# Self-attention of a routed transformer layer: keys rotated ahead of queries, norms in two parts, logits in other banks

## The reference

```python
x = x + xattn(layernorm(x), ctx)      # one head, 257 keys, width 384 to 512
x = x + attn(layernorm(x), ...)       # 16 heads of 32, rotary embedding, 32 keys
x = x + ffn(layernorm(x), ...)        # 8 experts of 1024, the best 2 per token
```

```python
q, k, v = x @ Wq.T + bq, x @ Wk.T + bk, x @ Wv.T + bv      # (B, T, 16, 32)
q, k = apply_rope(q), apply_rope(k)   # [x1*cos - x2*sin, x1*sin + x2*cos]
attn = softmax(einsum('bthd,bshd->bhts', q, k) / sqrt(32))
out = einsum('bhts,bshd->bthd', attn, v).reshape(B, T, C) @ Wo.T + bo
```

## Time and profile before

| what | value |
|---|---|
| median of 3 runs | 589.7 us (588.83 to 590.61) |
| the profiled execution, timed | 589.92 us |
| its span in the profile | 588.0 us |
| mean granted TensorE clock | 0.935 of full |
| busy: TensorE, VectorE, ScalarE, GpSimd | 506.1, 391.0, 285.9, 113.1 us |
| chain that ended last | TensorE 67%, VectorE 10%, issue 10%, ScalarE 5%, GpSimd 3%, DMA 3% |

### The profile page before, as it was taken

How to read it: one execution, slowest core, us unless ns; L and a number is a source line. 1 busy time by engine, 2 the same in 40 slices (tenths; PEclk the granted TensorE clock), 3 DMA queues, 4 the chain that set the end, 5 groups by cost and what they waited for, 6 DMA issues and landing times.

```text
span 588.0 us, 11090 instructions
## 1 busy us (share of the span) xinstructions
PE 506.1 (86%) x3601; PEld 294.6 (50%) x3602; DVE 391.0 (67%) x876; ACT 285.9 (49%) x449; POOL 113.1 (19%) x89
## 2 busy tenths in 40 slices
PE   5799999999989899886630699999999999999993
PEld 3664657474657576645330344445445444544441
DVE  2889778937977969698886566666563736673330
ACT  0652868686256464675720345454443525652120
POOL 1212114102232030300471001211211121121112
PEclk9799999999989989897855779999999999999998
DMA  8992505000008994125288157887585776744222
GB/s 326 390 382 87 216 1 215 2 1 2 1 0 303 379 382 172 37 80 208 90 299 294 44 174 223 267 255 237 107 262 132 218 214 154 232 93 90 54 54 37
DMA packets 54961, 98.74 MB, mean 168 GB/s; under 512 B 25072, under 2 KB 26256, under 8 KB 50832
## 3 DMA queue, kind: packets, MB, share of 16 engines
q1 hardware_dynamic: 23984, 74.81, 35.9%
q10 hardware_dynamic: 26640, 13.73, 9.5%
q0 software_dynamic: 4304, 9.77, 7.8%
HBM read 63.36 MB, written 29.43 MB: 158 GB/s over the span
## 4 chain that ended last, share of the span: by engine, by line
PE 67%; DVE 10%; issue 10%; ACT 5%; POOL 3%; DMA 3%; SPq 0%; ACTq 0%; POOLq 0%; DVEq 0%
PE bank L691 20%; PE bank L709 19%; PE bank L343 7%; PE bank L511 4%; PE bank L495 2%; PE bank L425 2%; PE bank L455 2%; PE bank L405 2%; PE bank L361 2%; PE bank L476 1%; PE bank L545 1%; ACT ctxT_region L737 1%; DMA routed_rows<-shared,ints 1%; POOL small L1544 1%; PE bank L604 1%
## 5 line engine op out<-in xcount | busy, mean ns | idle before, releaser
L691 PE MATMUL bank<-wbuf,ctx_region 128*128 x504 | 117.8, 393 | 6.3 <-issue 5.3
L1400 DVE SCALAR_TENSOR_TENSOR wbuf<-ctx_region,wbuf 128x2048 f32 (+1 forms) x28 | 62.9, 2288 | 31.9 <-ACT wbuf L876 31.9
L1642 POOL DMA_INDIRECT out<-misc,ints x21 | 38.6, 1840 | 230.2 <-ACT misc L957 175.0
L691 PEld LDWEIGHTS bank<-wbuf,ctx_region 128*128 128x128 f16 x504 | 49.4, 101 | 66.9 <-issue 15.5
L876 ACT ACTIVATE wbuf<-ctx_region 128x2048 f32 (+1 forms) x28 | 51.9, 1902 | 28.6 <-issue 26.2
L1544 POOL TENSOR_TENSOR small<-small 128x2 f32<-128x2 f32 (+2 forms) x25 | 27.7, 1109 | 190.8 <-DVE small L1030 184.2
L709 PE MATMUL bank<-wbuf,actT 128*128 x264 | 58.8, 379 | 1.0 <-DVE actT L1504 1.0
L976 ACT ACTIVATE ctxT_region<-bank 128x512 f32<-128x512 f32 x42 | 25.1, 597 | 69.6 <-PE bank L691 69.6
L709 PE MATMUL bank<-wbuf,xn 128*128 x240 | 53.4, 379 | 0.0
L511 PE MATMUL bank<-ctx_region,wbuf 128*128 128x256 f16 x384 | 45.2, 280 | 4.3 <-DVE ctx_region L1159 3.4
L511 PEld LDWEIGHTS bank<-ctx_region,wbuf 128*128 128x128 f16 x384 | 38.0, 100 | 12.0 <-DVE ctx_region L1159 4.1
(11 more groups left out here) (214 smaller groups left out, 823.4 us busy)
## 6 DMA issues: line engine op xcount, KB each, us to landing
ctx_region<-in_experts SPq DMA_DIRECT2D x28, 1024.0 KB, 5.4
routed_rows<-ctxT_region SPq DMA_DIRECT2D x1, 16900.0 KB, 50.6
ctx_region<-in_ctx SPq DMA_DIRECT2D x8, 1536.0 KB, 8.8
ctx_region<-routed_rows ACTq DMA_DIRECT2D x23, 260.0 KB, 3.6
wbuf<-in_experts SPq DMA_DIRECT2D x4, 1024.0 KB, 4.9
out<-x ACTq DMA_DIRECT2D x8, 256.0 KB, 2.5
x<-in_x SPq DMA_DIRECT2D x1, 1536.0 KB, 14.3
wbuf<-in_wqT SPq DMA_DIRECT2D x4, 256.0 KB, 4.3
```

What stands on the lines that cost most here:

```text
L691: mm = nc.tensor.matmul(bank[half][:, :], xgT[:, b, x_part, k * P:(k + 1) * P], w16[:, ds(at + (w_part + k * EH + half * 512), 512)], star ...
L1400: nc.vector.scalar_tensor_tensor(w16[:, ds(at + (LOW + n * PIECE), PIECE)], src_[:, piece], W_SCALE, w16[:, ds(at + (HIGH + n * PIECE), PI ...
L1642: nc.gpsimd.indirect_dma_start(out, bass.IndirectOffsetOnAxis(idx[:, slot_no:slot_no + 1].bitcast(U32), axis=0), y_out[:, slot_no, :], Non ...
```

## The change

On VectorE the keys of the next pair are rotated before its queries. `first_norm` is split in `first_stats`, ahead of the keys' rotation, and `first_scale`, behind it. The queries' shuffle and cosine (`turn_cos`) stand before `attended_low`, their sine (`turn_sin`) behind `normalised_low`, and their sum (`join`) between the statistics (`last_stats`) and the scaling (`last_scale`) of the last norm. `logits_out` stands behind the keys' rotation and the scaling, in the pass before the last behind both rotations. On TensorE the scores go ahead of `features_T`, and the values ahead of the logits; the first two pairs' logits go to banks 4 and 5. On ScalarE the exponentials come first, then the queries' copies, then the features'. Waits follow the new order: `scores` wait for both sums, `key_columns` for the first of the two, `values` for the feature copies, `attend` for the queries' copies, and the output products of passes 1 and 2 for the last pair's logits sum (z). The first pair keeps its order.

```diff
--- before.py
+++ after.py
@@ -43,7 +43,7 @@
 PIECE = EXPERT // W_PIECES
 ROW_SLOTS = 2
 ROUTED = ((0, TILES - 4), (TILES - 4, TILES - 2), (TILES - 2, TILES))
-LOGIT_BANK = (2, 2, 6, 2)
+LOGIT_BANK = (4, 4, 6, 2)
 COUNT_BANKS = ((0, 1), (0, 1), (0, 1))
 
 
@@ -525,6 +525,8 @@
 
             def values(pair):
                 pe.wait_ge(s["sw_lo"], 3)
+                if pair > 1:
+                    pe.wait_ge(s["xfT"], 2 * pair - 2)
                 if pair:
                     pe.wait_ge(s["sv"], 2 * pair)
                 else:
@@ -537,7 +539,7 @@
                     mm.then_inc(s["sv_ps"], 1)
 
             def scores(pair):
-                pe.wait_ge(s["rotated"], 2 * pair + 1)
+                pe.wait_ge(s["rotated"], 2 * pair + 2 if pair else 1)
                 pe.wait_ge(s["k_exp"], pair + 1)
                 for t in range(2):
                     for c4 in range(KC):
@@ -558,8 +560,8 @@
 
             def attend(pair):
 
-                if pair:
-                    pe.wait_ge(s["z"], min(2 * pair, TILES - 4))
+                if pair + 1 < PAIRS:
+                    pe.wait_ge(s["sq"], 2 * pair + 4)
                 for t in range(2):
                     pe.wait_ge(s["p_cols"], 2 * pair + t + 1)
                     pe.wait_ge(s["sv"], 2 * pair + t + 1)
@@ -577,6 +579,8 @@
                     normalised_T(pair + 2)
                 if pair == 0:
                     pe.wait_ge(s["sw_lo"], 4)
+                elif pair + 1 < PAIRS:
+                    pe.wait_ge(s["z"], 2 * pair)
                 for t in range(2):
                     pe.wait_ge(s["ao_hi"], 2 * pair + t + 1)
                     for k in range(KC):
@@ -597,7 +601,7 @@
 
             def logits(pair):
                 if pair + 2 < PAIRS:
-                    pe.wait_ge(s["sq"], 2 * pair + 6)
+                    pe.wait_ge(s["sk"], 2 * pair + 6)
                 for t in range(2):
                     pe.wait_ge(s["xfT"], 2 * pair + t + 1)
                     for k in range(KC):
@@ -647,13 +651,13 @@
                     logits(pair - 1)
                 else:
                     queries(pair + 1)
+                    scores(pair)
                     if pair:
                         features_T(pair - 1)
-                    scores(pair)
                     keys(pair + 1)
+                    values(pair + 1)
                     if pair:
                         logits(pair - 1)
-                    values(pair + 1)
                 attend(pair)
             pe.wait_ge(s["z"], TILES - 2)
             features_T(PAIRS - 1)
@@ -883,7 +887,7 @@
 
             def key_columns(pair):
 
-                act.wait_ge(s["rotated"], 2 * pair + 2)
+                act.wait_ge(s["rotated"], 2 * pair + 1 if pair else 2)
                 for r in range(4):
                     part = slice(r * HD, (r + 1) * HD)
                     op = nc.scalar.copy(k_exp[part, :, :, r, :], kbuf[part].rearrange("p (c b l) -> p c b l", c=KC, l=L))
@@ -908,22 +912,22 @@
             key_columns(0)
             for pair in range(PAIRS):
                 last = pair + 1 == PAIRS
+                if last:
+                    gate_exp(0)
+                for t in range(2):
+                    act.wait_ge(s["s_sub"], 2 * pair + t + 1)
+                    nc.scalar.activation(soft[:, t, :], soft[:, t, :], ACT.Exp, scale=H_SCALE).then_inc(s["s_exp"], 1)
+                if not last:
+                    turned_out(pair + 1)
                 if pair and not last:
                     features_out(pair - 1)
                     features_high(pair - 1)
-                if not last:
-                    turned_out(pair + 1)
-                for t in range(2):
-                    act.wait_ge(s["s_sub"], 2 * pair + t + 1)
-                    nc.scalar.activation(soft[:, t, :], soft[:, t, :], ACT.Exp, scale=H_SCALE).then_inc(s["s_exp"], 1)
                 if last:
                     features_out(pair - 1)
                     probs_out(pair)
                 else:
                     biased(k_T, 4, s["sk_ps"], 2 * pair + 2, "sbk", s["sk"])
                     probs_out(pair)
-                    if pair + 2 == PAIRS:
-                        gate_exp(0)
                     values_out(pair + 1)
                 for t in range(2):
                     act.wait_ge(s["ao_ps"], 2 * pair + t + 1)
@@ -1035,14 +1039,6 @@
             def x_at(tile):
                 return x[:, tile * D:(tile + 1) * D]
 
-            def norm_pair(srcs, dsts, name, pair):
-                norm_stats(srcs, stats, mv, ve, s[f"{name}_ve"])
-                dve.wait_ge(s[f"{name}_rstd"], pair + 1)
-                out_sem = s[f"{name}_out"]
-                for t in range(2):
-                    normalise(dsts[t], srcs[t], mv[:, t, 0:1], rstd[:, t:t + 1]).then_inc(out_sem, 1)
-                dve.wait_ge(out_sem, 2 * pair + 2)
-
             count(nc.vector.memset(neg_half, -0.5), "route", wait=False)
             dve.wait_ge(s["x_in0"], 16)
 
@@ -1146,11 +1142,21 @@
                     nc.vector.tensor_tensor(x2a[:, 1, :, tile_at], x2aT[:, :, tile_at], x2a[:, 0, :, tile_at], ALU.subtract)\
                         .then_inc(s["x2a_lo"], 1)
 
-            def first_norm(pair):
+            def first_stats(pair):
+                dve.wait_ge(s["x_new"], 2 * pair + 2)
+                norm_stats([x_at(2 * pair), x_at(2 * pair + 1)], stats, mv, ve, s["ln3_ve"])
+
+            def first_scale(pair):
+                dve.wait_ge(s["ln3_rstd"], pair + 1)
                 if pair == 0:
                     dve.wait_ge(s["x1T_ps"], TILES)
-                dve.wait_ge(s["x_new"], 2 * pair + 2)
-                norm_pair([x_at(2 * pair), x_at(2 * pair + 1)], [xn[:, 0, :], xn[:, 1, :]], "ln3", pair)
+                for t in range(2):
+                    normalise(xn[:, t, :], x_at(2 * pair + t), mv[:, t, 0:1], rstd[:, t:t + 1]).then_inc(s["ln3_out"], 1)
+                dve.wait_ge(s["ln3_out"], 2 * pair + 2)
+
+            def first_norm(pair):
+                first_stats(pair)
+                first_scale(pair)
 
             def normalised_low(pair):
                 for t in range(2):
@@ -1268,19 +1274,30 @@
             cos_t = const("cos")[:, None, :].to_broadcast(table)
             turned = ((qb, q_sw, s["sq"]), (kbuf, k_sw, s["sk"]))
 
-            def turn(pair, n):
+            def nth(pair, n):
+
+                return 2 * pair + (2 - n if pair else n + 1)
+
+            def turn_cos(pair, n):
 
                 buf, sw, ready = turned[n]
                 dve.wait_ge(ready, 2 * pair + 2)
                 nc.vector.stream_shuffle(sw, buf, swap).then_inc(s["swapped"], 1)
-                dve.wait_ge(s["swapped"], 2 * pair + n + 1)
+                dve.wait_ge(s["swapped"], nth(pair, n))
                 nc.vector.tensor_tensor(by_place(buf), by_place(buf), cos_t, ALU.mult).then_inc(s["cosined"], 1)
+
+            def turn_sin(n):
+                sw = turned[n][1]
                 nc.vector.tensor_tensor(by_place(sw), by_place(sw), sin_t, ALU.mult).then_inc(s["sined"], 1)
+
+            def turn(pair, n):
+                turn_cos(pair, n)
+                turn_sin(n)
 
             def join(pair, n):
                 buf, sw, _ = turned[n]
-                dve.wait_ge(s["cosined"], 2 * pair + n + 1)
-                dve.wait_ge(s["sined"], 2 * pair + n + 1)
+                dve.wait_ge(s["cosined"], nth(pair, n))
+                dve.wait_ge(s["sined"], nth(pair, n))
                 nc.vector.tensor_tensor(buf, buf, sw, ALU.add).then_inc(s["rotated"], 1)
 
             def attended_low(pair):
@@ -1312,7 +1329,7 @@
                         dve.wait_ge(s["p_cols"], 2 * pair + t - 1)
                     nc.vector.transpose(soft_T[:, t, :], soft[:, t, :]).then_inc(s["s_pT"], 1)
 
-            def last_norm(pair):
+            def last_stats(pair):
 
                 for t in range(2):
                     tile = 2 * pair + t
@@ -1323,6 +1340,8 @@
                     dve.wait_ge(s["x_post"], tile + 1)
                     count(nc.vector.bn_stats(stats[:, t, :], x_at(tile)), "norm_step", wait=(t == 1))
                 norm_mean(stats, mv, ve, s["ln4_ve"], 2)
+
+            def last_scale(pair):
                 dve.wait_ge(s["ln4_rstd"], pair + 1)
                 if pair:
                     dve.wait_ge(s["xf_lo"], 2 * pair)
@@ -1415,24 +1434,30 @@
                 softmax(pair)
                 if last:
                     choose(0)
+                if pair + 2 < PAIRS:
+                    first_stats(pair + 2)
+                if not last:
+                    turn(pair + 1, 1)
+                    join(pair + 1, 1)
+                if pair + 2 < PAIRS:
+                    first_scale(pair + 2)
+                if pair + 2 == PAIRS:
+                    turn(pair + 1, 0)
+                    join(pair + 1, 0)
                 if pair:
                     logits_out(pair - 1)
                 if pair + 2 < PAIRS:
-                    first_norm(pair + 2)
-                if not last:
```

(14 more changed lines are left out.)

## The result

The changed kernel takes 585.05 us (median of 18 runs, 582.57 to 586.34) against 588.73 us for the kernel before (18 runs, 585.29 to 591.7): ratio 0.9939, with a 95% interval of [0.9918, 0.996], 3.6 us faster. The forecast was 583.5, the range 581.0 to 586.8. The profiled execution took 584.41 us, with a mean granted clock of 0.937.

The account below looks back on a forecast made before the run. Bound: TensorE idle stretches of 2.88 us, waiting on a normalisation, then slow-clock scores in two passes; VectorE bounds the third. Terms: -7.6 + 1.4 = -6.2; 589.92 - 6.2 = 583.7, median 583.5 us; range 581.0 to 586.8.

Parts of the forecast that it names:

- Pass 0: First pass: keys rotated first delay transposes and low-part products; pair 2's queries' products start 1.5 us later, at 200.4.
- that just fits: Pass 1: VectorE has L1290's first tile at 225.7 us, TensorE wants it at 225.6; pair 3's queries stay -3.0.
- The new wait: Pass 2: output products wait for VectorE's logits sum, starting at 253.9 us after 2.3 us of TensorE idle time.
- The clock term: Pass 2: clock falls behind the 2.3 us idle stretch before the output products, costing 1.4 us; chance 0.42.
- the clock holds: Rival: full clock behind all the new TensorE gaps, gain 7.6 us, 582.1 us; chance 0.30.
- 2.49 was enough: Clock argument: 1.2 GHz followed a 2.49 us idle stretch at 169.80, so the nearby 2.3 us in pass 2 would too.
- moves as a block: Everything behind self-attention (choosing, scattering rows, expert loop) hangs in one chain, unchanged in length and about 6 us earlier.
- the last pass, which keeps its order: Last self-attention pass: listed as costing nothing, its order being unchanged.
- At no cost: List of free items: moved attend waits, gate_exp's move, values waiting for feature copies, the last pass; no DMA added.
- VectorE was not stalled: Rival: GpSimd's low-part subtractions stall VectorE 2.1 us in pass 1; 585.6 us; chance 0.20, shared with late key copies.
- the slower case: Rival: key rotation waits for ScalarE's key copies behind output writes' issues; 5 us a pass gives 592 us; chance 0.04.
- Nothing won: Rival: scores wait for the queries' sum, 3 us late in both passes, as long as for the norm; 589.7 us; chance 0.04.

Follow-up runs that it names:

- e3: Changed kernel with TensorE's scores again behind the features' transposes, VectorE's and ScalarE's orders and banks staying changed: 588.54 us, ratio 0.9993 to the kernel before.
- e6: Changed kernel with ScalarE's old order, exponentials again behind the features' and queries' copies: 591.71 us, ratio 1.0046 to the kernel before.
- e7: Changed kernel with low parts ahead of the queries' cosine in passes 0 and 1, first_scale inside the key rotation: 584.27 us, ratio 0.9934 to before.
- before's third profile: The kernel before, unedited, profiled a third time: 590.45 us (1 run).
- before's second: The kernel before, unedited, profiled again: 586.66 us (1 run).
- e2: Kernel before with only TensorE's scores moved ahead of the features' transposes, VectorE and ScalarE in old order: 593.84 us, ratio 1.0067.
- e1: Kernel before with 12 useless TensorE products filling the idle stretches ahead of the features' transposes in passes 1 and 2: 588.47 us, ratio 0.9987.
- e9: e8 with the last pair's low parts of the features subtracted on VectorE instead of GpSimd: 577.26 us, ratio 0.9778 to the kernel before.
- e5: Changed kernel with useless products filling TensorE's idle stretches in passes 2 and 3: 584.02 us, ratio 0.9927 to the kernel before.
- e8: Changed kernel with pass 2's logits in banks 0 and 1, and first_scale and the low parts moved ahead: 581.88 us, ratio 0.9849 to before.

## Why the prediction was right, and where it was off

**The path was right to within 0.6 us at each point** of the first profile (in the second every point is 1.0 to 1.1 us later, as is the first scores):

| TensorE starts | forecast | measured |
|---|---|---|
| pair 2's queries | 200.4 | 200.51 |
| pass 1's keys | 208.7 | 208.66 |
| pair 3's queries | 229.1 | 229.33 |
| pass 2's keys | 237.4 | 237.47 |
| pass 2's output products | 253.9 | 254.48 |
| last pass's scores | 259.2 | 259.75 |

Pass 0 cost about what was worked out (+1.6 by the clock of the trace, +1.2 counted from the first scores, which were 0.4 us later already; idle 1.43 and 1.25 us). In pass 1 the queries' sum was done at 204.6, ahead of the scores; "that just fits" was 0.30 us short. The root of pass 1's last norm was less well hidden than forecast: it ran beside the queries' sum and took 1.61 us in place of 0.70, and the scaling waited 0.59 us for it. That cost nothing, as the transposes no longer stand ahead of the scores. (The 0.71 us of the earlier trace rows is how long the root took; the wait for it was 0.8 us.) The 0.6 us in pass 2 are ScalarE's last key copies, which held VectorE for 0.96 us until 244.19 against 243.6 forecast.

**The new wait** was right in kind and place (L1355 releases the output products), with 2.85 us in place of 2.3.

**The clock term** (+1.4) did not come where it was put. Behind the 2.85 us the products took 1.89 us in both profiles of the changed kernel, so for that place the rival "the clock holds" was right. It fell there in e3 (3.78 us) and e6 (4.77 us) and held in e7 (3.16 us). The argument "2.49 was enough, so 2.3 is near it" read three places of one profile as a rule; before's third profile breaks it at 2.88 us, before's second at the 2.49 us themselves. Nor was 1.84 us a safe length: the clock was low behind 1.95 us in e6 and 2.17 us in e2.

**The step that failed** is the first paragraph's: everything behind self-attention "moves as a block", and with it "the last pass, which keeps its order", which stands under "At no cost". Between the mean of before's three profiles and that of the changed kernel's two, the four parts differ by +0.9, -7.0, +2.8 and -0.6 us, together -4.0, near the 3.6 of the medians. The first part lies ahead of everything that the change moves, so its 0.9 are chance. So 7.0 of the 7.6 us came, and 2.8 went again in the third part, for which the sum had no term:

- From the last scores to the last choices it was 36.4, 36.2 and 37.2 us before, 38.6 and 37.1 after. No wait on that way is new. What differs most is how long the last pass's output products stay at the lower clock. Their first eight took 1.89, 1.89 and 2.39 us before, and 3.60 (above) and 2.26 in the changed kernel. Up to the products of the choice just ahead of them it is the same to 0.2 us. The other profiles sort by VectorE's order, with which the logits' banks change: with the old one (e1, e2) 1.89 us, with the new one (e3 to e9) 2.22 to 3.60 us. So all nine profiles with the new order have the slow stretch and one of five with the old order. This is a price of the clock, at a place where I had put none; its mean over many executions is not measured.
- From the last choices to the first expert rows it was 20.1, 18.7 and 21.5 us before, 21.2 and 22.2 after. That is the landing of the scattered rows beside the expert loads; before's own values differ by 2.8 us, so this share (some 1.6 us) may well be chance.

**Luck, and a dear reference.** The 1.4 us booked for a fall of the clock that did not come stood in, by luck, for half of the loss that was not in the sum; without it the forecast would have been 582.1 us. The forecast was also counted from 589.7 us, where the median of all 18 runs is 588.73; from there it would have been 582.5 us, 2.5 under the measured time. And it started from an execution of 589.92 us. In it both idle stretches were followed by a slow one: 1.20 + 0.39 + 1.34 + 0.29 = 3.2 us over the full-speed durations. I booked all of it as saved. In before's third profile it was 1.6 us, and e1, whose profile shows none of it, gained 0.7 us in the median.

**The rivals.** VectorE was not stalled. GpSimd's subtractions ran at 213.42 us in the changed kernel, mostly beside VectorE operations with one input, as the case against that rival said; GpSimd's and VectorE's timelines:

```profile
213.42 2.39 POOL L1617 TENSOR_TENSOR shared<-misc,shared 128x512 f16<-128x512 f32 x2 [4.61 <-ACT shared L867]
...
213.70 0.71 DVE L1330 STREAM_TRANSPOSE misc<-ctxT_region 128x512 f32<-128x512 f32 x1
214.34 1.24 DVE L1028 BATCH_NORM_STATS2 small<-x 128x6 f32<-128x512 f32 x2
```

The last operation of the softmax with two inputs (212.97 to 213.66 us) overlapped their start by 0.24 us and was no longer for it; the next of that kind, the key rotation's cosine, started at 217.34 us, 1.5 us behind them. VectorE met a stall only where it had met one before, at the last choice (now 2.75 us for L1372). Key copies behind the output writes' issues came 0.6 us later than forecast in one pass (VectorE waited 0.96 us for them), far from the 5 us at which the slower case would have begun. "Nothing won" needed a late queries' sum; it was in time.

**What stays open:** the mean price of the clock in either kernel, to some 1 us (a profile shows one execution of many), why the last pass's products stay slow longer in VectorE's new order, how much of the third part is chance, and what the scores and the exponentials moved without the keys would give.

## What to carry to other kernels

When a later stage is kept waiting by a chain through another engine, move what heads that chain (here the scores, and with them the softmax), and move all engines' orders together: TensorE's alone cost 3.9 us, the others without it won nothing, and ScalarE's was worth 6.3. When a product moves behind another, look at what stands behind its copy in the next engine's queue. Forecast structure from the rows, but read slow-clock stretches from several profiles before booking them as saved, and expect part of a gain to be lost in the stretches behind it. Look at what GpSimd runs beside VectorE at the end of a chain: moving one subtraction that sat on it brought the last choice 2.0 us earlier, and the kernel with it was 4.6 us faster.

## What the runs showed of the hardware that was not expected

- The same 2.88 us idle stretch of TensorE, in the same kernel, was followed by scores of 3.57, 3.29 or 1.95 us, and one of 2.49 us by the lower clock in seven profiles of fourteen. Idle stretches of 2.85 and 3.16 us were followed by full speed, of 1.95, 2.17, 3.78 and 4.77 us by half. The length of the idle stretch alone did not tell the clock behind it.
- A higher mean granted clock (0.947 in e5 against 0.940 in the changed kernel's second profile) brought no time that could be measured.
- A VectorE comparison with two SBUF inputs waited for two GpSimd subtractions: 2.66 us (e8) against 0.29 without them (e9), though by the records it started 0.22 us ahead of them (starts on GpSimd are rough). The Trainium skill ("SBUF — State Buffer", Who interferes with whom) has the two exclude each other for a whole instruction; here VectorE did not get in between the two subtractions.
- GpSimd waits for VectorE as well: its root (L1569), begun 0.16 us behind the queries' sum, took 1.61 us in the changed kernel and 0.70 before, where nothing with two SBUF inputs ran beside it.
